# Four products of 32 output rows in place of one wide product, in a four-layer attention kernel

## What is computed

```python
q = proj(query, Wq, bq)
k = proj(key_, Wk, bk)
v = proj(value, Wv, bv)
scores = jnp.einsum('bshd,bkhd->bhsk', q, k) * scale
attn = jax.nn.softmax(scores, axis=-1)
o = jnp.einsum('bhsk,bkhd->bshd', attn, v).reshape(B, S, D_MODEL)
```

## Time and profile before

| | |
|---|---|
| median of 3 runs | 1116.84 us (1113.83 to 1118.72) |
| profiled execution | 1119.34 us, span 1117.6 us |
| mean granted TensorE clock | 0.960 of 2.4 GHz |
| TensorE matmuls, busy | 1000.5 us (90%), 9658 records |
| TensorE weight loads, busy | 554.8 us (50%), 9658 |
| VectorE | 818.8 us (73%), 1687 |
| ScalarE | 762.0 us (68%), 1692 |
| GpSimd | 414.7 us (37%), 411 |
| mean DMA rate | 65 GB/s |

### The profile page before, as it was taken

How to read it: one execution, slowest core, us unless ns; L and a number is a source line. 1 busy time by engine, 2 the same in 40 slices (tenths; PEclk the granted TensorE clock), 3 DMA queues, 4 the chain that set the end, 5 groups by cost and what they waited for, 6 DMA issues and landing times.

```text
span 1117.6 us, 25480 instructions
## 1 busy us (share of the span) xinstructions
PE 1000.5 (90%) x9658; PEld 554.8 (50%) x9658; DVE 818.8 (73%) x1687; ACT 762.0 (68%) x1692; POOL 414.7 (37%) x411
## 2 busy tenths in 40 slices
PE   0579999999989999999998999999999999998996
PEld 0235555555545555555454555555555545454442
DVE  5697787788767778887887776767677777676851
ACT  1157777876768787878777666666666675757675
POOL 5865545545412341334124142424333342423100
PEclk9979999999999999999999898989898989899999
DMA  8232212321222232223222120202020212111100
GB/s 211 67 94 81 75 52 64 81 72 50 82 63 68 82 105 66 79 81 102 70 81 79 30 80 19 81 18 81 18 83 19 82 36 65 45 55 54 31 4 5
DMA packets 64449, 72.98 MB, mean 65 GB/s; under 512 B 8210, under 2 KB 59994, under 8 KB 64198
## 3 DMA queue, kind: packets, MB, share of 16 engines
q1 hardware_dynamic: 64326, 71.33, 22.7%
HBM read 50.35 MB, written 18.15 MB: 61 GB/s over the span
## 4 chain that ended last, share of the span: by engine, by line
PE 62%; DVE 21%; ACT 8%; issue 5%; POOL 2%; SPq 1%; DMA 0%; POOLq 0%; ACTq 0%; DVEq 0%
PE acc L733 16%; PE ring L674 15%; PE sexp L713 14%; DVE mx L1105 6%; DVE mneg L1111 4%; DVE mx L1103 3%; PE ring L607 3%; PE ring L619 3%; ACT probs L981 2%; PE ring L797 2%; ACT kp L927 2%; PE ring L648 2%; DVE max L1206 1%; SPq L462 1%; ACT sc L1006 1%
## 5 line engine op out<-in xcount | busy, mean ns | idle before, releaser
L1105 DVE TENSOR_TENSOR mx<-ring,mx 120x400 f16<-120x400 f32 (+1 forms) x1056 | 554.5, 567 | 197.0 <-PE ring L674 194.7
L981 ACT ACTIVATE probs<-sexp 120x400 f32<-120x400 f32 (+1 forms) x1152 | 539.6, 513 | 197.5 <-PE sexp L713 192.6
L674 PE MATMUL ring<-qx,krep 96*128 96x400 f16 (+2 forms) x1152 | 398.7, 351 | 43.0 <-ACT kp L927 14.6
L713 PE MATMUL sexp<-qx,krep 97*128 97x400 f16 (+2 forms) x1152 | 396.3, 348 | 8.8 <-ACT probs L981 5.0
L733 PE MATMUL acc<-probs,vx 120*18 120x200 f32 (+1 forms) x4608 | 258.7, 343 | 0.8 <-ACT probs L981 0.7
L713 PEld LDWEIGHTS sexp<-qx,krep 97*128 97x128 f16 (+2 forms) x1152 | 127.0, 111 | 141.1 <-ACT probs L981 79.7
L674 PEld LDWEIGHTS ring<-qx,krep 96*128 96x128 f16 (+2 forms) x1152 | 127.7, 111 | 128.1 <-DVE mx L1105 30.9
L733 PEld LDWEIGHTS acc<-probs,vx 120*18 120x18 f32 (+1 forms) x4608 | 108.0, 98 | 115.7 <-issue 81.8
L481 POOL TENSOR_TENSOR kp<-kf,kp 128x480 f16<-128x480 f32 (+1 forms) x72 | 79.4, 1108 | 204.6 <-ACT kp L927 204.6
L519 POOL TENSOR_TENSOR qx<-qs,headmask 96x400 f16<-96x400 f16 x96 | 80.1, 864 | 54.1 <-PE sexp L713 30.3
L498 POOL TENSOR_TENSOR rstd<-vare,half 100x1 f32<-100x1 f32 x24 | 13.0, 543 | 214.3 <-DVE vare L1122 214.3
(11 more groups left out here) (131 smaller groups left out, 906.4 us busy)
## 6 DMA issues: line engine op xcount, KB each, us to landing
krep<-kept SPq DMA_DIRECT2D x144, 120.0 KB, 2.6
ctf<-in_ctxT SPq DMA_DIRECT2D x16, 722.0 KB
kept<-kp SPq DMA_DIRECT2D x48, 240.0 KB, 2.7
krep<-kept SPq DMA_DIRECT2D x72, 121.0 KB, 3.0
kept<-kp SPq DMA_DIRECT2D x24, 242.0 KB, 2.5
nat<-in_ctx SPq DMA_DIRECT2D x8, 720.0 KB
maskexp<-maskmax SPq DMA_DIRECT2D x8, 281.2 KB, 3.4
anymask<-in_mask SPq DMA_DIRECT2D x1, 1128.1 KB, 7.2
```

What stands on the lines that cost most here:

```text
L674: last = pe.matmul(ps[0:n, 0:QW], krep[0:PARTS, u.par, t, c0:c0 + n], qx[0:PARTS, u.third, t, :, :].rearrange("p f s -> p (f s)"), start=T ...
L713: last = pe.matmul(ps[0:n, 0:QW], krep[:, u.par, t, c0:c0 + n], qx[:, u.third, t, :, :].rearrange("p f s -> p (f s)"), start=True, stop=no ...
L981: act.activation(probs[0:r, j % PR, :], sexp[j % SR][0:r, 0:QW], ACT.Exp).then_inc(sem["probs_ready"], 1)
L1105: op = dve.tensor_tensor(dst, src, dst, ALU.max)
```

## The change

A helper `grouped` splits the output rows of a product into pieces of 32 (the last may be smaller) and issues one product for each, with the matching 32 columns of the stationary operand and the same moving tile. It is put around nearly all products that had more than 32 output rows. The f32 transposes at L637, L744, L750, L761, L787 and L805 become products with the identity as the moving operand, also in pieces. Unchanged are the context transposes (L596), the mask transposes (L629), the transposes of `mx` (L689), of `mneg` (L697), the `acc` products (L733), the small queries of layer 2 (L769) and the values of layer 2 (L797). Only the last piece increments the semaphore. Nothing changes on the other engines. In the changed kernel the numbers of lines behind the helper move up by 7 to 12, and all the pieces have the helper's line, L583.

```diff
@@ -576,6 +576,13 @@
+        def grouped(run, out, w, x, **flags):
+
+            for g in range(0, out.shape[0], 32):
+                m = min(32, out.shape[0] - g)
+                last = run(out[g:g + m], w[:, g:g + m], x, **flags)
+            return last
+
@@ -604,8 +611,8 @@
                 for j, (w, c) in enumerate(((0, 0), (0, 1), (1, 0))):
-                    last = pe.matmul(ps[:, 0:n], wk16[:, w, u.L, :], ct[:, u.par, c, c0:c0 + n], start=(j == 0),
-                                     stop=(j == 2))
+                    last = grouped(pe.matmul, ps[:, 0:n], wk16[:, w, u.L, :], ct[:, u.par, c, c0:c0 + n], start=(j == 0),
+                                   stop=(j == 2), skip_group_check=True)
             def vals(u, g):
@@ -616,8 +623,8 @@
                 for i, c in enumerate(groups()[g][0]):
                     for j, (w, p) in enumerate(((0, 0), (1, 0), (0, 1))):
-                        last = pe.matmul(ps[0:r, D * i:D * i + D], ct[:, u.par, p, c0:c0 + r], wv16[:, w, u.L, :],
-                                         start=(j == 0), stop=(j == 2))
+                        last = grouped(pe.matmul, ps[0:r, D * i:D * i + D], ct[:, u.par, p, c0:c0 + r], wv16[:, w, u.L, :],
+                                       start=(j == 0), stop=(j == 2), skip_group_check=True)
@@ -634,7 +641,7 @@
-                pe.transpose(ps[:, 0:S], xcur[:, :], ident[0:S, 0:S]).then_inc(sem["xT_filled"], 1)
+                grouped(pe.matmul, ps[:, 0:S], xcur[:, :], ident[0:S, 0:S], start=True, stop=True).then_inc(sem["xT_filled"], 1)
             def queries(u):
@@ -643,17 +650,18 @@
-                    pe.matmul(ps[0:PARTS, 0:T * S], bq16[:, u.L, :], which16[:, :], start=True, stop=False, skip_group_check=True)
+                    grouped(pe.matmul, ps[0:PARTS, 0:T * S], bq16[:, u.L, :], which16[:, :], start=True, stop=False,
+                            skip_group_check=True)
                 for t in range(T):
-                    last = pe.matmul(ps[0:PARTS, S * t:S * t + S], wq[:, u.L, t, :], xT[:, :], start=not u.L, stop=True,
-                                     skip_group_check=u.L > 0)
+                    last = grouped(pe.matmul, ps[0:PARTS, S * t:S * t + S], wq[:, u.L, t, :], xT[:, :], start=not u.L,
+                                   stop=True, skip_group_check=u.L > 0)
             def add_mask(ps, tile, which, c, r):
-                return pe.matmul(ps.rearrange("p (h s) -> p h s", h=HT), masked_by[0:r, which, 0:r],
-                                 tile[0:r, c, :].unsqueeze(1).broadcast_to([r, HT, S]), start=False, stop=True,
-                                 skip_group_check=True)
+                return grouped(pe.matmul, ps.rearrange("p (h s) -> p h s", h=HT), masked_by[0:r, which, 0:r],
+                               tile[0:r, c, :].unsqueeze(1).broadcast_to([r, HT, S]), start=False, stop=True,
+                               skip_group_check=True)
@@ -671,9 +679,9 @@
-                last = pe.matmul(ps[0:n, 0:QW], krep[0:PARTS, u.par, t, c0:c0 + n],
-                                 qx[0:PARTS, u.third, t, :, :].rearrange("p f s -> p (f s)"),
-                                 start=True, stop=not masks, skip_group_check=masks)
+                last = grouped(pe.matmul, ps[0:n, 0:QW], krep[0:PARTS, u.par, t, c0:c0 + n],
+                               qx[0:PARTS, u.third, t, :, :].rearrange("p f s -> p (f s)"),
+                               start=True, stop=not masks, skip_group_check=masks)
@@ -710,9 +718,9 @@
-                last = pe.matmul(ps[0:n, 0:QW], krep[:, u.par, t, c0:c0 + n],
-                                 qx[:, u.third, t, :, :].rearrange("p f s -> p (f s)"),
-                                 start=True, stop=not masks, skip_group_check=masks)
+                last = grouped(pe.matmul, ps[0:n, 0:QW], krep[:, u.par, t, c0:c0 + n],
+                               qx[:, u.third, t, :, :].rearrange("p f s -> p (f s)"),
+                               start=True, stop=not masks, skip_group_check=masks)
@@ -741,42 +749,43 @@
                 for t in range(T):
-                    last = pe.transpose(ps[0:S, 128 * t:128 * t + 128], osb[:, S * t:S * t + S], ident[:, :])
+                    last = grouped(pe.matmul, ps[0:S, 128 * t:128 * t + 128], osb[:, S * t:S * t + S], ident[:, :], start=True,
+                                   stop=True)
             def output_back(u):
-                pe.transpose(ps[:, 0:S], oatt[:, 0, :], ident[0:S, 0:S]).then_inc(sem["oT_filled"], 1)
+                grouped(pe.matmul, ps[:, 0:S], oatt[:, 0, :], ident[0:S, 0:S], start=True, stop=True).then_inc(sem["oT_filled"], 1)
             def project(u):
-                pe.matmul(ps[0:S, 0:D], oT[:, :], wo[:, u.L, :], start=True, stop=True).then_inc(sem["wo_filled"], 1)
+                grouped(pe.matmul, ps[0:S, 0:D], oT[:, :], wo[:, u.L, :], start=True, stop=True).then_inc(sem["wo_filled"], 1)
...
             def scores2(u, t):
-                pe.matmul(ps[0:S, 0:QW], q2[:, :], kbd2[:, HT * t:HT * t + HT, :].rearrange("p h s -> p (h s)"),
-                          start=True, stop=True).then_inc(sem["s2_filled"], 1)
+                grouped(pe.matmul, ps[0:S, 0:QW], q2[:, :], kbd2[:, HT * t:HT * t + HT, :].rearrange("p h s -> p (h s)"),
+                        start=True, stop=True).then_inc(sem["s2_filled"], 1)
             def transposed2(u, t):
@@ -784,7 +793,8 @@
                 for h in range(HT):
-                    last = pe.transpose(ps[0:S, S * h:S * h + S], sc2[:, HT * t + h, :], ident[0:S, 0:S])
+                    last = grouped(pe.matmul, ps[0:S, S * h:S * h + S], sc2[:, HT * t + h, :], ident[0:S, 0:S], start=True,
+                                   stop=True)
@@ -802,20 +812,22 @@
-                pe.transpose(ps[:, 0:S], att2[:, :], ident[0:S, 0:S]).then_inc(sem["at2_filled"], 1)
+                grouped(pe.matmul, ps[:, 0:S], att2[:, :], ident[0:S, 0:S], start=True, stop=True).then_inc(sem["at2_filled"], 1)
             def hidden2(u):
                 for j in range(FF // 128):
-                    last = pe.matmul(ps[:, S * j:S * j + S], w1[:, 128 * j:128 * j + 128], aT2[:, :], start=True, stop=True)
+                    last = grouped(pe.matmul, ps[:, S * j:S * j + S], w1[:, 128 * j:128 * j + 128], aT2[:, :], start=True,
+                                   stop=True)
...
```

11 lines of the change are left out of this document (6 added, 5 removed).

## The result

The changed kernel takes 1127.32 us (median of 4 runs, 1124.75 to 1131.77) against 1115.42 us of the kernel before on the same chip: ratio 1.0095, 95% interval 1.0066 to 1.0124. It is slower by about 1%, where 1106 us was forecast. The profiled execution took 1124.75 us, that of before 1119.34, so the two traces hold 5 of the 12 us: the traced execution lies 2.6 us under the median in the changed kernel and 3.9 over it in the kernel before. The granted TensorE clock has a part in that: over the changed kernel's profiled execution it was 0.958, over its three others, all of 1127.3 us and more, 0.946 to 0.948, while the kernel before had 0.955 to 0.966 in 45 of the 46 executions that ran beside the experiments (1113.03 us at 0.966, 1124.54 at 0.957); the 46th, 1168.81 us at 0.838, was a disturbed one and counts nowhere.

What follows compares the result with a forecast made beforehand. The prediction took TensorE to bound the kernel (62% of the chain, plus 5% issue). TensorE's -43 + 26 - 5 = -21 us, three quarters felt (16), less 2 and 3, gave 11 us gained: 1106 us median, range 1087 to 1138.

Steps and rivals of the forecast that it cites:

- The price of a change of form: Entering and leaving column-strip form around each `acc` group on TensorE costs about 0.20 us, over 288 groups 57.6 us.
- rival D: Slower: strip weight loads stand exposed at score, V and key products, 68 us less 16, about 1169 us; chance 0.06.
- The islands: Wide pieces left between strips, mostly transposes and layer-2 values: 110 at 0.19 us each, 20.9 us new on TensorE.
- the transposes cost what was said: f32 transposes as identity products take two records: 26 us more on TensorE, L744's group of four 0.88 us, not 0.44.
- the sum on TensorE: TensorE's work: -43 for changes of form, +26 for transposes, -5 for shorter f32 weight loads, together -21 us.
- The 3 us for late strips: After a wait, a product's last strip starts later, delaying other engines about 120 times: 2 to 10 us, taken as 3.
- Rival E: Much faster: transposes as products keep the clock at 2.4 GHz in eight layer-2 stages, 1072 us; chance 0.08.
- I take 2 us, near the cheap end: Feeding TensorE the V products' extra instructions: nothing at 4 ns each, 35 us at 12 ns; 2 us taken.
- rival C: Slower: above 7 ns per instruction V groups become bound by instruction feed, +18 us, 1135 us; chance 0.16.
- 0.75 x 21: Three quarters of TensorE's 21 us reaches the end, since the chain lies on TensorE about that often: 16 us.
- hardly 0.4 us: Gain left in a 54 us stage where layer 2 runs, its 16 probability transposes eating the rest.
- Rival B: The gain is taken up by waits, such as for ScalarE's exponentials: within 5 us of 1117; chance 0.20.

Runs made afterwards that it cites:

- v_one_strips: The changed kernel with one of the three V products per chunk, still in strips (32 instructions per V group, not 96): 0.9847 of the kernel before.
- v_one: The kernel before with one of the three V products per chunk, no form changed: 0.9879 of the kernel before.
- together2: The kernel before, all wide, with `acc` products in groups of 8 in place of 16 (288 more groups): 1.0721 of the kernel before.
- t_wide: The changed kernel with the output transposes and the layer-2 probability transposes wide again: 0.9913 of the kernel before.
- v_wide: The changed kernel with only the V products wide again: 1118.51 us, 0.9998 of the kernel before.
- v_halves: The changed kernel with each V group issued in two halves, one step apart, and ScalarE's copy one step later: 1.0036 of the kernel before.
- combo: The changed kernel with V products and the output and layer-2 probability transposes both wide again: 0.9922 of the kernel before.
- combo_merged: combo with two wide pieces (third context transposes, first maxima's transposes) moved beside other wide pieces: 1105.5 us, 0.9902 of the kernel before.
- scores_only: The kernel before with strips for the two score products and the mask-adding products alone: 1.0081 of the kernel before.

## Why the prediction was wrong

**What held.** The price of a change of form was there and a little higher (0.25 us for an `acc` group, not 0.20). Strips run side by side at the rate of a wide product, so rival D is refuted, and the rule of the Trainium skill (TensorE: Matmul & The Clock Gate, Part 3, The mechanism) beside it, that a weight load overlaps running matmuls only when its row group differs, does not hold for these strips: score products of four strips with the same rows stand 0.17 us apart at 603 us, and that is the median of all 1402 such pairs at full clock. The islands were counted right (110), the transposes cost what was said (0.88 and 0.71 us), and the sum on TensorE, 21 us less, came out as 20.4 less busy. Part of that match is luck: 0.05 us more for each of 288 groups would make the sum 35, and the slower V groups, which the prediction kept out of the sum, are in the busy time. The 3 us for late strips were too many: in the 80 score products of the changed kernel that follow a wait of over 0.1 us, the last strip starts 0.01 us after the first, 1 us for 120 of them. Rival E didn't come: after the layer-2 values the clock falls as before. This stretch of the changed kernel shows 0.65 where the earlier trace rows had 0.55, but only because the stretch is cut otherwise; within it 0.50 lasts from 625.7 us past its end, 6.8 us in all as before:

```profile
623.40:631.00 7.60, 6.83 (x83) 4.04 (x86) 4.28 (x13) 2.33 (x6) 1.25 (x3) 0.65 0.07 16
```

**The first step that failed: the feed, "I take 2 us, near the cheap end".** The lead behind an `acc` group was argued from the pace of single instructions, between 4 and 12 ns. The pace that V groups show is 9.5 ns, inside that range and past the 7 ns at which the text lets rival C decide, so many V groups grew by 0.1 to 0.3 us in layers 0 and 1, and none in layer 3. But the larger part is of another kind: gaps of 1.3 to 2.0 us at four groups, and 3.2 us more at the branch, together most of 10.5 us more issue time, twice the 5.0 us by which the traces differ. Undoing the strips of V gave 11 us, and removed 17 us of idle time. The sign and the place were rival C's, the size was not: it had 35 us from a steady pace, and V groups of 1.0 us or more everywhere.

What the gaps are: most likely TensorE's instructions are not there. v_one_strips shows that they need the density, not the strips; the instruction queue carries one 16 KB packet per 253 added instructions; and all nine gaps of over 0.8 us at V groups in three kernels end 2.24 to 2.57 us after such a packet starts, while packets in this part of the changed kernel follow each other at 2.3 to 7.7 us. The gap behind the branch ends at the same distance in the kernel before (2.47 us). At 9.5 ns a block of 253 lasts 2.4 us, so a dense stretch can use one up before the next has come. That last link is inferred: the trace doesn't say for which engine a packet is, and no run changed the fetching alone. The Trainium skill (Runtime: NRT & Kernel Launch, Instruction fetch mechanics) gives blocks of 256 instructions, which agrees with the 253, and says of the cost of crossing into the next one that it is "mostly hidden". In the kernel before it was, but for the branch; in the changed one it was not at four V groups.

**The second: "0.75 x 21", the share that is felt.** It was taken as one number for gains and costs, from TensorE's share of the chain over the span. v_one measured it as 0.4: in full in layer 0, a third (0.48 of 1.35 us) in layer 1 and next to nothing (0.12 of 1.35 us) in layer 3, there with more of the stage at the lower clock. together2 has about half in layers 0 and 1. The gain on `acc` is spread over a unit's steps and met waits there. The cost of the transposes stands in layer 2's own chain, from exponentials to output, where the next link needs it: t_wide gave back 20 us by the medians (12.7 between the two traces, of which only 6.5 is TensorE's busy time), and the stages of layer 3, for which the prediction had "hardly 0.4 us" of gain, lost 1.25. With equal work in a stage (50.2 and 50.1 us), its length grew by 1.4. Undoing both kinds of transposes took 1.28 us off such a stage; the layer-2 ones alone are 4 x 0.32 us longer in it, which fits their length being felt about in full. The other kernels fit too: against before, the same stages are 0.63 to 0.83 us longer in the three others that keep these transposes in strips (v_wide, v_halves, v_one_strips), and -0.12 and +0.17 in combo and combo_merged, which don't; but scores_only, whose transposes are wide, has +0.60, and each of these means is good to 0.3 to 0.8 us only. L744 and L787 were undone together, not one by one, so how the 20 us split between them, and that it is this chain, is argued and not shown. Rival B had this mechanism with a price of nothing lost; it couldn't turn the sign, because it treated cost and gain alike.

**The third, small: the prologue.** The sum spread all terms over stages. Ahead of the first exponential no `acc` group runs, so there is no change of form to win, and islands and dense products only cost: +2.9 us. It may be less: together2, which has the same work there as the kernel before, shows +1.4 us, so prologues differ by that much by themselves.

The net is not a clean ledger, since the gains of undoing overlap (combo). Forecast and result lie 1.9% apart, 21 us. The first step accounts for about 9 of it (11 against 2, give or take 4). The rest goes by the stages to the second, as far as is known: gains on `acc` felt at about half or less, and more lost in layer 3 than the change in TensorE's work there. Between the traces the distance is 16 us (1124.75 against 1108.3); the other 5 are how the traced executions lie to their medians; the lower clock of the changed kernel's other three has a part in them, and its cause stays open.

## What to carry to other kernels

When column strips and full-width products alternate on TensorE, look at the "issue" time before the strips' loads: here a change to strips and back cost 0.25 us at full clock. Placing pieces of one form side by side removes it without more instructions; where that was tried (combo_merged), one of two places gained and the other didn't. Count instructions per microsecond in the densest stretch, not only their sum: products of 128 columns in four strips need 96 instructions in 0.67 us, and in layers 0 and 1 that ran dry at some groups. And don't weigh a gain that is spread over a loop with the same share as a cost that stands in a serial chain: cut one piece of work in a run of its own and see, stage by stage, what share of it is felt, with the granted clock of the stage beside it: where the clock differs, a share is not yet the share of the work.

## What the runs showed of the hardware

Four strips of one product, with the same rows and four different weights, take the time of one wide product (0.17 us for 400 columns at 603 us of the changed kernel) with their loads hidden. A change of form costs about 0.09 us in, 0.12 out and 0.05 between the next two wide products (together2). TensorE took 96 instructions in 0.91 us (9.5 ns each) in first V groups of layers 0 and 1 and in 0.67 us (7.0 ns each) in layer 3, and single gaps of 0.9 to 2.1 us in mid-product stand where 96 of them stand together; which unit is hit differs from kernel to kernel. Behind the branch on the mask flag TensorE stood 2.7 us in the kernel before and 3.4 and 2.5 us in the changed one. With 288 more changes of form, the granted clock from 600 to 800 us went down from 0.92 to 0.83.
